# Two pairs of result-less matmuls at the entry of the width-one attention, and an earlier copy of the last turned output

## What is computed

```python
    x = x + _L1_xattn_ref(_layernorm(x), ctx_1024, ctx_1024, ...)
    x = x + _L1_ffn_ref(_layernorm(x), ...)
    x = x + _L2_attn_ref(_layernorm(x), L2_attn_w_qkv, L2_attn_w_out)

def _L2_attn_ref(x, w_qkv, w_out):
    qkv = jnp.einsum('bnc,fc->bnf', x, w_qkv)
    q, k, v = jnp.split(qkv, 3, axis=-1)
    q, k, v = (t.transpose(0, 2, 1)[..., None] for t in (q, k, v))
    dots = jnp.einsum('bhid,bhjd->bhij', q, k) * scale
    attn = jax.nn.softmax(jnp.where(causal, dots, -jnp.inf), axis=-1)
    out = jnp.einsum('bhij,bhjd->bhid', attn, v)
    return jnp.einsum('bnh,ch->bnc', out[..., 0].transpose(0, 2, 1), w_out)
```

## Time and profile before

| | |
|---|---|
| median of 3 runs | 3161.09 us (3159.74 to 3161.25) |
| profiled execution, its own time | 3160.37 us |
| span of its trace | 3158.4 us |
| TensorE busy | 2935.1 us, 93% |
| VectorE busy | 1863.5 us, 59% |
| ScalarE busy | 1254.6 us, 40% |
| mean granted TensorE clock | 0.969 of full |
| chain that ended last | 77% TensorE, 17% VectorE, 4% ScalarE |

### The profile page before, as it was taken

One profiled execution on the slowest core, in us unless ns is written; L12 is line 12 of the kernel. 1 busy time (PEld: TensorE's weight loads), 2 busy tenths in 40 slices (PEclk: granted clock), 3 DMA queues, 4 the chain that ended last, 5 costly groups with the idle time before them and its releaser, 6 DMA issues.

```text
span 3158.4 us, 52225 instructions
## 1 busy us (share of the span) xinstructions
PE 2935.1 (93%) x20631; PEld 1955.1 (62%) x20671; DVE 1863.5 (59%) x6438; ACT 1254.6 (40%) x1944; POOL 431.8 (14%) x458
## 2 busy tenths in 40 slices
PE   7999999988989889988998999999999999998998
PEld 4666666865555556655665556566667766766653
DVE  5534443699999536875678787574244344434455
ACT  2222222335656433324443578554332333323443
POOL 0010010114343311000000256300000000000000
PEclk9999999999999999999999799899999999998999
DMA  3000000010000000000000011100000000000000
GB/s 129 1 1 0 1 1 1 1 53 1 2 1 2 34 33 1 1 2 4 2 1 5 24 36 28 42 1 27 1 1 0 1 1 1 0 1 9 2 1 27
DMA packets 22028, 37.75 MB, mean 12 GB/s; under 512 B 2132, under 2 KB 19733, under 8 KB 20760
## 3 DMA queue, kind: packets, MB, share of 16 engines
q1 hardware_dynamic: 20968, 34.02, 3.2%
q10 hardware_dynamic: 816, 0.39, 0.1%
HBM read 26.81 MB, written 2.10 MB: 9 GB/s over the span
## 4 chain that ended last, share of the span: by engine, by line
PE 77%; DVE 17%; ACT 4%; issue 2%; DMA 0%; DVEq 0%; SPq 0%; POOL 0%; ACTq 0%; POOLq 0%
PE ps L415 45%; DVE arena L568 3%; PE ps L620 2%; PE ps L688 2%; PE ps L3053 2%; PE ps L3072 2%; ACT arena L674 2%; PE ps L1603 2%; PE ps L2369 2%; PE ps L2323 2%; PE ps L516 2%; DVE arena L1937 2%; PE ps L729 2%; PE ps L2926 1%; PE ps L553 1%
## 5 line engine op out<-in xcount | busy, mean ns | idle before, releaser
L415 PE MATMUL ps<-weights,arena 128*128 128x256 f32 (+4 forms) x2480 | 692.2, 428 | 43.1 <-DVE arena L1818 26.1
L415 PEld LDWEIGHTS ps<-weights,arena 128*128 128x128 f32 (+1 forms) x2480 | 460.8, 195 | 209.9 <-issue 93.7
L415 PE MATMUL ps<-arena,weights 128*128 128x256 f32 (+4 forms) x1726 | 560.8, 473 | 13.7 <-DMA weights<-in_w_L_attn 5.8
L415 PEld LDWEIGHTS ps<-arena,weights 128*128 128x128 f32 (+1 forms) x1726 | 316.2, 191 | 217.7 <-issue 157.4
L415 PE MATMUL ps<-arena 128*128 128x256 f32 (+4 forms) x1618 | 426.2, 416 | 6.0 <-ACT arena L4771 1.5
L415 PEld LDWEIGHTS ps<-arena 128*128 128x128 f32 (+2 forms) x1618 | 298.0, 188 | 115.0 <-issue 74.9
L568 DVE TENSOR_REDUCE arena<-ps 128x16 f32<-128x1232 f32 (+2 forms) x96 | 179.1, 1865 | 150.6 <-PE ps L546 51.7
L674 ACT ACTIVATE arena<-ps 77x2048 f32<-77x2048 f32 (+1 forms) x112 | 210.1, 1876 | 124.6 <-PE ps L620 62.8
L1937 DVE MATCH_REPLACE8 arena<-arena 128x77 f32<-128x77 f32 x1024 | 214.3, 224 | 0.0
L2336 ACT ACTIVATE arena<-ps 128x1536 f32<-128x1536 f32 x128 | 185.7, 1452 | 57.4 <-PE ps L2325 50.5
L857 POOL TENSOR_TENSOR x<-x,weights 128x512 f32<-128x512 f32 x32 | 43.9, 1372 | 1195.2 <-DVE arena L823 1148.6
(11 more groups left out here) (427 smaller groups left out, 4432.7 us busy)
## 6 DMA issues: line engine op xcount, KB each, us to landing
arena<-arena SPq DMA_DIRECT2D x156, 32.0 KB
weights<-in_w_L_ffn SPq DMA_DIRECT2D x1, 3848.0 KB, 11.5
weights<-in_w_L_attn SPq DMA_DIRECT2D x1, 3840.0 KB, 15.0
weights<-in_w_L_xattn SPq DMA_DIRECT2D x3, 1024.0 KB, 6.3
weights<-in_w_L_ffn SPq DMA_DIRECT2D x1, 3072.0 KB, 10.5
x<-in_x SPq DMA_DIRECT2D x2, 1024.0 KB
weights<-in_w_L_xattn SPq DMA_DIRECT2D x1, 2048.0 KB, 7.4
out<-x SPq DMA_DIRECT2D x8, 256.0 KB, 2.2
```

The source lines that it names most:

```text
L415: ins = k.nc.tensor.matmul(out, lhsT, rhs, start=start and i == 0, stop=i == n - 1)
```

## The change

Two edits. TensorE gets a helper that issues n matmuls of 128x128 weights and 512 columns on the context, into a bank that nobody reads before it is overwritten: a pair into bank 3 after the wait for v, ahead of group 0's scores, and a pair into bank 0 behind group 2's scores, after a wait for the exponential of group 1 that frees the bank, ahead of the wait for the means and the turn. VectorE's copy of bank 7 to x.oT goes from behind the mask of group 5 to behind the mask of group 3, ahead of the bound's last three steps.

```diff
+def awake_tensor(k, b, n):
+
+    for _ in range(n):
+        k.nc.tensor.matmul(k.ps[:, b, :], k.ctxT[:, 0, 0:P], k.ctxT[:, 0, 0:512], start=True, stop=True)
@@ L2_attn_tensor
             if n == 0 and g == 0:
                 pe.wait_ge(*s.sig.at("v", 0, 0, 1))
+                awake_tensor(k, 3, 2)
...
             if n == 0 and g == 2:
+                pe.wait_ge(*s.sig.at("prob", 0, 0, 2))
+                awake_tensor(k, 0, 2)
                 after(pe, x, left, "o")
                 fp8_turn_tensor(k, pe, x, older, 7)
@@ L2_attn_vector
+            if n == 0 and g == 3:
+                after(dve, x, left, "oT_ps")
+                k.nc.vector.tensor_copy(flat(x.oT), k.ps[:, 7, :]).then_inc(*x.sig.up("c_oT"))
             if n == 0 and g in (2, 3):
                 for i in (0, 1) if g == 2 else (2, 3, 4):
                     step_bound_vector(k, dve, s, 1, i)
-            if n == 0 and g == 5:
-                after(dve, x, left, "oT_ps")
-                k.nc.vector.tensor_copy(flat(x.oT), k.ps[:, 7, :]).then_inc(*x.sig.up("c_oT"))
```

## The result

The changed kernel is slower: 3179.93 us as the median of 22 executions (3163.93 to 3189.06), against 3162.01 us of before (22 executions on the same chips, 3158.30 to 3182.53). The ratio is 1.0034, with a 95% interval of 1.0019 to 1.0048; it is the quotient of the two means (3176.7 and 3166.0 us), where the quotient of the medians is 1.0057. The prediction was 3154.6 us.

A forecast was written before the change was run, and what follows sets the result against it. TensorE, busy 93% of the span, was taken to be bound by its low clock from 1752.40 to 1769.4 us; full clock there would save 6.5 us: 3161.1 - 6.5 = 3154.6 us, range 3150 to 3164.

The forecast's parts named there:

- The first pair: Fillers ahead of group 0's scores: end near 1744.7 us, scores 0.3 us late, at no cost thanks to 2 us cover.
- A: The forecast case: at the stage's entry the clock stays or is back before 1756; 6.5 us less, 3154.6 us; chance 0.50.
- C: Rival: clock falls between the pairs, second pair at 1.2 GHz, turn 1.2 us late, low stretch stays; 3162.3 us; chance 0.27.
- The gain at group 7: Sequence 0, group 7's mask: 5.8 to 6.8 us sooner; 5.3 to 5.8 if the clock is back only near 1755.6.
- the 6.5 us of the sum: Entry gain taken: TensorE's upper end of 7.8 us, less a good microsecond because VectorE is late next.
- The moved copy: VectorE's copy ahead of the output product: saves up to 2 us at high clock, already in the 6.5; nothing at low.
- After group 7 both kernels do the same work at the same clock: Rest of the kernel behind sequence 0's group 7: nothing differs, so the 6.5 us reach the end.
- D of the rivals: Rival: copy neutral, pairs fit, VectorE takes TensorE's gain back in groups 8 to 15; 3160.5 us; chance 0.08.
- Rival B: Second dip, after 1795 us, also changes: none gives 3148 us, a longer one 3157; chance 0.15.
- The matmuls of 1748 to 1752: Window with the second pair: some 2.4 us of matmuls instead of 1.86, an argument that the clock stays.
- VectorE's walk: VectorE's remaining work up to group 7's mask: would end at 1766.0, or 1765.3 with overlaps, so mask 5.8 to 6.8 us sooner.
- the line: 0.2% of the time, 6.3 us: about what a measurement of this kernel can tell from no change.

The follow-up runs named there:

- e3_first: The change without its second filler pair (first pair and moved copy kept): 3165.72 us, ratio to before 1.0017.
- e4_second: The change without its first filler pair (second pair and moved copy kept): 3177.62 us, ratio to before 1.0031.
- g2_best: The change plus fillers at further waits in sequences 0, 1 and 2, four of them at sequence 1's group 8: 3149.06 us, ratio to before 0.9942.
- e1_fillers: The change with the copy of bank 7 put back behind group 5's mask, both filler pairs kept: 3176.33 us, ratio to before 1.0017.
- e2_copy: The change without either filler pair, only the moved copy: 3160.67 us, ratio to before 1.0000.
- g1_third_n1: The change plus single fillers in groups 10 and 13 of sequence 1 and a pair at sequence 0's group 8: 3160.44 us, ratio to before 0.9985.
- e5_thin: The change with fillers using 32 of the array's 128 rows: 3170.60 us, ratio to before 1.0015.
- f1_n1: The kernel before plus one filler each in groups 10 and 13 of sequence 1: 3161.68 us, ratio to before 0.9977.

## Why the prediction was wrong

Range and sign were both missed: 3179.9 against 3154.6 (3150 to 3164), slower where a chance of 0.04 was given.

**The first pair** was right but for its worth. Predicted to start at 1742.95 and take 1.76 us; it took 1.98 from 1743.11 and cost nothing. The clock held through 1744 to 1748. Alone it is worth nothing (e3_first).

**The clock.** A named two ways: it stays, or it is back before 1756. The second came: it fell after the first pair, at 1748.5, and was back at 1755.4. C said that after a fall the second pair would not bring it back; e4_second shows that it does, in 3.78 us at 1.2 GHz (predicted 3.5, with the turn at 1753.6; measured 1753.9).

**The gain at group 7**, 5.3 to 5.8 us in this case, was 3.9: the 6.5 us of the sum were mis-sized before anything took them back. VectorE was named as late next, and it was; the walk was some 1.5 us too generous. With a clean clock (g2_best) it is 5.9, inside the 5.8 to 6.8 given for that.

**The moved copy** was put at up to 2 us at the high clock. It is worth 3.7 us there, since without it the wait becomes 3.52 us long, and the clock falls as it ends (e1_fillers). At the low clock it is worth nothing, as said (e2_copy).

**The step that failed** is the sentence "After group 7 both kernels do the same work at the same clock", from which followed "So the 6.5 us reach the end". The work is the same, the clock is not. The projection behind L1119 waited 0.52 us in before; with TensorE ahead and VectorE not, the wait became 2.10 us, and the clock fell as it ended, for 14 us: the 3.9 us gained became 2.3 us lost at group 15. With this wait filled and nothing else changed (g1_third_n1) they stayed a gain, of 3.9 us. D of the rivals was set aside with the same argument, "those groups are the same in both".

**Rival B** had the right mechanism at the wrong place and size: "a dip some microseconds longer takes about 2 us back". It looked only at the dip after 1795. Its argument against itself, that the wait of 1.75 us there stays, did not hold: the change's wait is 0.26 us, and the dip came all the same, at 1799.8, with the same 20 us. In the change's timeline of TensorE:

```profile
1799.37 0.77 PE L2375 MATMUL ps<-arena 128*32 128x256 f32 x8 [0.26 <-DVE arena L2351]
```

The stretch near 1769 took 6.2 us, and that after 1830 another 14.9 in the profiled execution.

**The spread** was read from three runs, 3159.7 to 3161.3, and so the question of what the change does to an execution's chance of the long stretch was never asked. In before it is 6 of 22 here and 39 of 117 over all runs; in the change 14 of 22. The two fillers ahead of 1830 show that it hangs on that place.

**Its working.** Three figures do not follow from their own terms. The matmuls of 1748 to 1752 would be 2.7 us (half of 1.86, and 1.8 of the pair) where it has 2.4, and g2_best, with a clean clock, has 3.08. VectorE's walk gives 5.8 to 6.5 us for the mask, not 5.8 to 6.8. B puts 0.07 beyond the line where a third of 0.15 is 0.05. None of them moves the forecast.

**What stays open.** Why one execution of a program takes the stretch after 1830 and the next does not: the wait for L2623 in before, after which the clock stayed, is as long as the change's for L2632, after which it fell, as the two rows of the last section show. Which of the two waits ahead of it opens it, if a wait does: both got a filler in every run that had one. And why the change makes it more frequent, if it is not in part chance: the fillers alone, whose profiled execution is before's after group 7, have 7 of 12 above 3173 (before on that chip 10 of 35), so a shift of the waits by the sooner entry is not needed for it. Of the excess of the median, 17.9 us, 6 to 8 us lie within each group; the rest is that the median execution has moved from the lower to the upper group. No lower execution of the change was profiled. The nearest is e4_second's, 4.9 us of span over before's: 2.9 us of that are there at the last mask and 1.8 come behind it, which no run explains.

## What to carry to other kernels

An idle wait of TensorE can cost the low-clock stretch that follows it, and not its own length: a wait of 2.10 us was followed by a stretch that cost 6.2 us. Whoever makes TensorE come sooner at one place must therefore look at its next waits, since they can grow by what was gained (0.52 us became 2.10, none became 4.12), and fill those too; fillers at one entry alone made this kernel slower, fillers at nine places made it 0.6% faster. The length of a wait does not tell by itself what follows: after 1.16 us the clock stayed in one trace and fell in another, and it fell after 0.26 us too. And three executions do not show a time with two values: compare the whole list, and check on which side the profiled one lies.

## What the hardware showed that was not expected

- Fillers over 32 rows, as long as those over 128, did not hold the clock: it was 0.50 in a window with TensorE busy for 4.00 of 4.00 us (e5_thin).
- One program has executions at about 3161 and at about 3174 us on one core. The wait ahead of the long stretch is equal in two traces whose clocks differ: TensorE's timeline of before, whose clock was 1.00 from 1828 to 1836, and of the change, whose clock fell to 0.50.

```profile
1827.26 0.41 PE L2411 MATMUL ps<-ident,arena 128*64 128x128 f32 x2 [1.16 <-DVE arena L2623]
```

```profile
1829.68 0.41 PE L2417 MATMUL ps<-ident,arena 128*64 128x128 f32 x2 [1.16 <-DVE arena L2632]
```

- One execution of f1_n1 took 11556 us, with a granted clock of 0.2 to 0.3 late in it, below the two levels that all other traces show. Its 128x512 f32 records took 2.7 us each (8 in 21.50 us from 1761.92) where the granted clock still reads 1.00, against 0.44 us in the earlier trace rows, so the clock does not account for all of it.
